# Graph network on Trainium2: in the gate layer, gather two of eight edge tiles on TensorE instead of by indirect DMA

## What is computed

```python
edge_input = jnp.concatenate([x[src], edge_attr], axis=-1)          # 100000 x (96 + 32)
messages = _gelu(edge_input @ mW1 + mb1) @ mW2 + mb2
gates = jax.nn.sigmoid(_gelu(edge_input @ gW1 + gb1) @ gW2 + gb2)
aggregated = jax.ops.segment_sum(messages * gates, dst, num_segments=x.shape[0])
update = _gelu(jnp.concatenate([x, aggregated], -1) @ uW1 + ub1) @ uW2 + ub2
# then x + update, layer norm, scale and shift
```

## Time and profile before

| what | us |
|---|---|
| median of 3 runs (3452.3 to 3453.14) | 3453.06 |
| the profiled execution | 3451.42 |
| its span, first to last instruction | 3449.7 |
| busy in the span: PE / DVE / POOL / ACT | 2703.8 / 2096.9 / 1316.5 / 692.8 |
| gate layer, from its first POOL instruction to the end of the span | 2371.2 to 3449.7 |
| 784 gathers on POOL (L1282): busy, and idle before them | 757.6, 243.8 |

### The profile page before, as it was taken

The page is one execution under the profiler, slowest core; times in us unless marked ns, Lnnn a source line. Parts: engine busy times, 40 slices in busy tenths (PEclk is TensorE's granted clock), DMA queues, the critical chain, the costliest instruction groups (busy, mean ns, idle before and its releaser), DMA issues.

```text
span 3449.7 us, 65375 instructions
## 1 busy us (share of the span) xinstructions
PE 2703.8 (78%) x22345; PEld 2109.0 (61%) x22346; DVE 2096.9 (61%) x4939; ACT 692.8 (20%) x1119; POOL 1316.5 (38%) x1350
## 2 busy tenths in 40 slices
PE   3677777999999989887999999985667765666764
PEld 0121111899999987776999999973445443444442
DVE  6888777823323472347988888874454545454545
ACT  0134455500000040111111111111111111111111
POOL 0000000000000000004777777753777777777772
PEclk9999999799999989998999999986776678776676
DMA  0000000000000000003544454522333333333331
GB/s 28 0 0 0 0 0 0 3 2 2 2 2 2 2 5 1 1 6 84 131 118 117 116 118 116 118 56 72 90 92 90 91 90 92 90 92 90 90 89 24
DMA packets 106162, 182.80 MB, mean 53 GB/s; under 512 B 37382, under 2 KB 65595, under 8 KB 105914
## 3 DMA queue, kind: packets, MB, share of 16 engines
q0 software_dynamic: 54880, 103.65, 12.1%
q1 hardware_dynamic: 51033, 75.67, 8.1%
HBM read 174.42 MB, written 4.80 MB: 52 GB/s over the span
## 4 chain that ended last, share of the span: by engine, by line
POOL 34%; issue 11%; DVE 5%; PE 2%; DMA 1%; ACT 0%; DVEq 0%; POOLq 0%; ACTq 0%
POOL gate_rows L1282 22%; POOL msg_rows L946 12%; DVE pre_space L1021 2%; PE msg_sums L1143 1%; DVE msg_rows L1045 0%; DMA first_rows<-pre_space 0%; PE gate_sums L1453 0%; ACT msg_src_near L958 0%; DVE pre_space L1350 0%; DVE msg_rows L1041 0%; DMA msg_rows<-h_rows,all_src_i 0%; DMA msg_src_row<-src_rows 0%; PE msg_sums L1158 0%; DVE pre_space L1113 0%; DMA gate_rows<-first_rows,all_src_i 0%
## 5 line engine op out<-in xcount | busy, mean ns | idle before, releaser
L1282 POOL DMA_INDIRECT gate_rows<-first_rows,all_src_i x784 | 757.6, 966 | 243.8 <-issue 238.7
L933 POOL MEMSET msg_shift<- 125x1 f32 x1 | 0.1, 100 | 1587.4 <-POOLq L646 1587.4
L946 POOL DMA_INDIRECT msg_rows<-h_rows,all_src_i x539 | 537.3, 997 | 164.1 <-issue 163.5
L1143 PE MATMUL msg_sums<-msg_parts,pre_space 125*128 125x192 f16 x6125 | 531.9, 249 | 36.3 <-DVE pre_space L1021 36.3
L1143 PEld LDWEIGHTS msg_sums<-msg_parts,pre_space 125*128 125x128 f16 x6125 | 513.0, 99 | 43.4 <-DVE pre_space L1021 37.8
L1453 PE MATMUL gate_sums<-gate_onehot,gate_passed 128*97 128x64 f32 x1584 | 257.2, 347 | 357.2 <-DVE gate_onehot L1380 357.2
L576 PE MATMUL hop_sums<-dense_work,dense_counts 125*128 125x192 f16 x6250 | 521.9, 247 | 14.3 <-DVE dense_t L530 6.7
L576 PEld LDWEIGHTS hop_sums<-dense_work,dense_counts 125*128 125x128 f16 x6250 | 519.2, 98 | 16.8 <-DVE dense_t L530 7.3
L1453 PEld LDWEIGHTS gate_sums<-gate_onehot,gate_passed 128*97 128x97 f32 x1584 | 239.4, 256 | 440.6 <-DVE gate_onehot L1380 440.5
L1344 DVE TENSOR_TENSOR gate_rows<-gate_rows,gate_sums 128x1536 f32<-128x1536 f32 x98 | 171.9, 1755 | 450.6 <-DMA gate_rows<-first_rows,all_src_i 450.6
L419 PE MATMUL cnt_sums<-cnt_hot,cnt_near 128*128 x1000 | 347.6, 411 | 119.3 <-DVE cnt_hot L358 114.3
(11 more groups left out here) (240 smaller groups left out, 2788.5 us busy)
## 6 DMA issues: line engine op xcount, KB each, us to landing
msg_edge<-edges SPq DMA_DIRECT2D x98, 384.0 KB
msg_src_row<-src_rows SPq DMA_DIRECT2D x49, 312.5 KB
gate_edge<-edges SPq DMA_DIRECT2D x98, 128.0 KB, 2.1
gate_rows<-first_rows,all_src_i POOLq DMA_INDIRECT x784
msg_rows<-h_rows,all_src_i POOLq DMA_INDIRECT x539
first_rows<-pre_space SPq DMA_DIRECT2D x6, 375.0 KB
all_x<-x SPq DMA_DIRECT2D x1, 1171.9 KB
h_rows<-all_h SPq DMA_DIRECT2D x6, 187.5 KB
```

The source lines that it names most:

```text
L946: nc.gpsimd.indirect_dma_start(out=rows[:, r, k, :], out_offset=None, in_=table, in_offset=bass.IndirectOffsetOnAxis(ap=src_i[:, at:at + 1 ...
L1143: last = nc.tensor.matmul(got[group % 2][:, n, 0:2 * D], pick[:, c % 2, j, i * EP:(i + 1) * EP], parts[:, j, :], start=(j == 0), stop=(j = ...
L1282: nc.gpsimd.indirect_dma_start(out=rows[:, r, k, :], out_offset=None, in_=table, in_offset=bass.IndirectOffsetOnAxis(ap=src_i[:, at:at + 1 ...
```

## The change

Of the 8 tiles of a group only 6 (BY) are still gathered by POOL from the table. The other 2 (ON) are gathered on PE, two groups (4 tiles, 512 edges) at a time: the picks are now the moving operand, so that the result is h of the sources, transposed, 96 x 512. ACT copies it under the 32 edge features, which SP loads to rows 96 to 127 of the same buffer `inputs`. PE then multiplies this 128-row input by the whole first weights `w1` on top of a bias product. ACT reads these two tiles for Gelu straight from PSUM, in instructions of their own. The edge product of the other six tiles becomes 2 x 3 matmuls with 96 rows and 192 columns, into one set of 3 banks instead of two. The picks have one buffer, in two parts of 13 and 12 node tiles (CUT). `parts`, `middle`, `node_no` and `w1` move to or appear in memory that both layers share. In the convolutions the six semaphores of the weight and bias loads become one, so that the first use waits for all six loads.

```diff
 # convolutions
-            for i in range(3):
-                sp.dma_start(w_sb[:, i, :], weights[i]).then_inc(w_loaded[i], 16)
...
+                sp.dma_start(w_sb[:, i, :], weights[i]).then_inc(loaded, 16)
+                sp.dma_start(b_sb[:, i, :], biases[i].unsqueeze(0).to_broadcast([NP, D])).then_inc(loaded, 16)
...
-                pe.wait_ge(w_loaded[c], 16)
+                pe.wait_ge(loaded, 96)
 # gated_layer, SP
+            for c in range(2):
+                load_row(c)
+                load_on_edges(c)
             for group in range(SLOTS):
                 load_edges(group)
+            load_row(2)
             for group in range(SLOTS, NG):
                 sp.wait_ge(edge_mixed, group - SLOTS + 1)
                 load_edges(group)
+                c = group // 2 + 1
+                if group % 2 and c < NG // 2:
+                    load_on_edges(c)
+                if group % 2 and c + 1 < NG // 2:
+                    load_row(c + 1)
 # POOL
-                for k in range(GT):
+                for k in range(BY):
 # ACT
+            def collect(c):
+                act.wait_ge(gathered, 2 * (c + 1))
+                if c >= 2:
+                    act.wait_ge(on_mixed, 2 * (c - 1))
+                nc.scalar.activation(inputs[0:D, c % 2, :], collected[c % 2], ACT.Copy).then_inc(collected_out, 1)
             def activate(group):
...
+                act.wait_ge(on_mixed, group + 1)
...
+                nc.scalar.activation(gated[:, group % 2, BY:GT, :], product[:, :, D:2 * D], ACT.Gelu
+                                     ).then_inc(gate_in, 1)
...
+                nc.scalar.activation(passed[:, group % KEPT, BY:GT, 0:D], product[:, :, 0:D], ACT.Gelu
+                                     ).then_inc(on_used, 1)
+                act.wait_ge(added, group + 1)
+                nc.scalar.activation(gated[:, group % 2, 0:BY, :], r[:, :, D:2 * D], ACT.Gelu).then_inc(gate_in, 1)
...
+            widen(0)
+            widen(1)
+            nc.scalar.activation(parts[:, :, 0:D], h[:, :, :], ACT.Copy, scale=ROW_LIFT).then_inc(rounded, 1)
+            widen(2)
+            collect(0)
 # DVE
+            def make_picks(c, part):
+                j0, j1 = ((0, CUT), (CUT, NT))[part]
+                if part == 0:
+                    dve.wait_ge(widened, c + 1)
+                if c:
+                    dve.wait_ge(gathered, 2 * (c - 1) + part + 1)
+                for j in range(j0, j1):
+                    nc.vector.tensor_scalar(pick[:, j, :], src_near[:, c % 2, :], node_no[:, j:j + 1],
+                                            1.0 / ROW_LIFT, ALU.is_equal, ALU.mult).then_inc(picked, 1)
+            make_picks(0, 0)
+            make_picks(0, 1)
...
+            make_picks(1, 0)
+            make_picks(1, 1)
             for turn in range(NG + 2):
...
                 if turn > 1:
                     steps = make_onehots(turn - 2)
+                if (turn + 4) // 2 < NG // 2:
+                    make_picks((turn + 4) // 2, turn % 2)
 # PE
+                if group:
+                    pe.wait_ge(added, group)
+                for half in range(2):
+                    for k in range(3):
+                        last = nc.tensor.matmul(sums[:, k, 2 * D * half:2 * D * (half + 1)],
+                                                edge[:, group % SLOTS, half, :], we[:, 2 * D * k:2 * D * (k + 1)],
+                                                start=True, stop=True)
...
+            def collect(c, part):
+                pe.wait_ge(picked, NT * c + (CUT, NT)[part])
+                if c >= 2:
+                    pe.wait_ge(collected_out, c - 1)
+                for j in range(*((0, CUT), (CUT, NT))[part]):
+                    for i in range(2):
+                        last = nc.tensor.matmul(collected[c % 2], parts[:, j, i * D:(i + 1) * D], pick[:, j, :],
+                                                start=(j == 0 and i == 0), stop=(j == NT - 1 and i == 1))
+                last.then_inc(gathered, 1)
+            def mix_inputs(group):
+                c = group // 2
+                pe.wait_ge(collected_out, c + 1)
+                pe.wait_ge(on_edge_ready[c % 2], 16 * (c // 2 + 1))
+                if group:
+                    pe.wait_ge(on_used, group)
+                nc.tensor.matmul(product, ones[:, :], bias[:, :, :], start=True, stop=False)
+                for i in range(ON):
+                    at = (group % 2 * ON + i) * EP
+                    last = nc.tensor.matmul(product[:, i, :], inputs[:, c % 2, at:at + EP], w1[:, :],
+                                            start=False, stop=(i == ON - 1))
+                last.then_inc(on_mixed, 1)
...
             for turn in range(NG + 2):
                 if turn + 1 < NG:
                     mix_edges(turn + 1)
+                if (turn + 3) // 2 < NG // 2:
+                    collect((turn + 3) // 2, (turn + 1) % 2)
+                if turn + 1 < NG:
+                    mix_inputs(turn + 1)
                 if turn > 1:
                     sum_messages(turn - 2)
```

More of the change, by code:

```diff
@@ L654, in convolutions @@
         sums = m.ps("sums", [128, 8, BANK], F32)
-        w_loaded = [m.sem(f"w_loaded{i}") for i in range(3)]
-        b_loaded = [m.sem(f"b_loaded{i}") for i in range(3)]
+        loaded = m.sem("loaded")
         chain = m.sem("chain"); normal = m.sem("normal")
@@ L919, in _ @@
                     sp.wait_ge(pre.we_cleared, 1)
-                    for k in range(4):
+                    for k in range(3):
                         at = 2 * D * k
@@ L1244, in gated_layer @@
         edge_ready = [m.sem(f"edge_ready{r}") for r in range(SLOTS)]
+        on_edge_ready = [m.sem(f"on_edge_ready{i}") for i in range(2)]
+        row_loaded = [m.sem(f"row_loaded{i}") for i in range(2)]
+        widened = m.sem("widened"); picked = m.sem("picked"); gathered = m.sem("gathered")
+        rounded = m.sem("rounded"); split = m.sem("split"); bias_set = m.sem("bias_set")
+        collected_out = m.sem("collected_out"); on_mixed = m.sem("on_mixed"); on_used = m.sem("on_used")
         edge_mixed = m.sem("edge_mixed"); added = m.sem("added"); rows_used = m.sem("rows_used")
@@ L1273, in _ @@
             nc.gpsimd.memset(passed[:, :, :, D:D + 1], 1.0).then_inc(made, 1)
+            nc.gpsimd.memset(ones[:, :], 1.0).then_inc(made, 1)
+            nc.gpsimd.memset(bias[:, :, :], 0.0).then_inc(made, 1)
             for i in range(2):
@@ L1319, in _ @@
                     open_gates(turn - 1)
+                if turn % 2 and (turn + 5) // 2 < NG // 2:
+                    widen((turn + 5) // 2)
+                if turn % 2 == 0 and (turn + 2) // 2 < NG // 2:
+                    collect((turn + 2) // 2)
             for q, (m0, n) in enumerate(GROUPS):
@@ new lines, in _ @@
+            link(nc.vector.tensor_copy(bias_part[:, 1, :], bias_rest[:, 0, :]))
+            link(nc.vector.tensor_tensor(bias_rest[:, 1, :], bias_rest[:, 0, :], bias_part[:, 1, :], ALU.subtract))
+            for k in range(ON):
+                link(nc.vector.tensor_copy(bias[0:1, k, :], b1[0:1, :]))
+                link(nc.vector.tensor_copy(bias[32:33, k, :], bias_rest[32:33, 0, :]))
+                link(nc.vector.tensor_copy(bias[64:65, k, :], bias_rest[64:65, 1, :]))
+            dve.sem_inc(bias_set, 1)
@@ L1337, in add_edges @@
             def add_edges(group):
                 turn, r = divmod(group, RING)
-                dve.wait_ge(rows_ready[r], 16 * GT * (turn + 1))
+                dve.wait_ge(rows_ready[r], 16 * BY * (turn + 1))
                 dve.wait_ge(edge_mixed, group + 1)
-                to = rows[:, r, :, :].rearrange("p k d -> p (k d)")
-                b = 3 * (group % 2)
-                products = sums[:, b:b + 3, :].rearrange("p b w -> p (b w)")
+                to = rows[:, r, :, :].rearrange("p (h k) d -> p h k d", h=2)
@@ L1344, in add_edges @@
+                products = sums[:, 0:3, 0:4 * D].rearrange("p k (h d) -> p h k d", h=2)
                 nc.vector.tensor_tensor(to, to, products, ALU.add).then_inc(added, 1)
@@ L1436, in mix_edges @@
                 pe.wait_ge(edge_ready[group % SLOTS], 16 * (group // SLOTS + 1))
-                if group >= 2:
-                    pe.wait_ge(added, group - 1)
-                b, wide, split = 3 * (group % 2), 4 * 2 * D, BANK // 2
-                for half, bank, to, frm, end in ((0, b, 0, 0, BANK), (0, b + 1, 0, BANK, wide),
-                                                 (1, b + 1, split, 0, split), (1, b + 2, 0, split, wide)):
-                    last = nc.tensor.matmul(sums[:, bank, to:to + end - frm], edge[:, group % SLOTS, half, :],
-                                            we[:, frm:end], start=True, stop=True)
@@ L1458, in _ @@
             mix_edges(0)
+            pe.wait_ge(joined_out, 2)
+            pe.wait_ge(split, 1)
+            collect(0, 0)
+            collect(0, 1)
+            pe.wait_ge(bias_set, 1)
+            mix_inputs(0)
+            collect(1, 0)
```

102 lines of the change are left out of this document (72 added, 30 removed).

## The result

The changed kernel takes 3400.39 us (median of 4 runs, 3395.86 to 3404.56) against 3452.68 us for the kernel before in runs beside it: ratio 0.9847, 95% interval 0.9835 to 0.986, about 53 us faster. The forecast was 3392 us. The profiled execution took 3397.08 us (3390.4 forecast), with a span of 3394.9 us and a granted clock of 0.95 over the whole.

A forecast was written before the change was run, and what follows sets the result against it. The gate layer was taken as bound by POOL's issue, 8 x 1.27 us a turn, then by PE. 63.5 us gained less 2.5 in the convolutions gave 61 off 3451.42: 3390.4, median 3392 us, range 3356 to 3432.

The forecast's parts named there:

- What sets the turn: Gate layer loop: PE sets the turn at 9.46 us, 9.54 with the clock allowance; PE never waits, DVE waits 0.3 us.
- The allowance of 0.08 us for half-clock spells: Gate layer loop: 0.08 us added to each PE turn for short spells at half clock.
- The price of a gather matmul: Gate layer, PE: a 512-column matmul costs 0.216 us, so half of 50 take 5.40 us a turn.
- the rival of a cheap PE: 512-column matmuls stream faster, so DVE's 9.15 us sets the turn: 36 us less, 3356 us; chance 0.05.
- DVE's turn: Gate layer loop: DVE needs 9.15 us a turn, with 12.5 picks of 0.285 us, 3.56 us in all.
- off the path as forecast: Gate layer, POOL: six gathers at 0.995 us busy beside picks, with their pauses, stay under 7.8 us a turn.
- The clock: Gate layer loop: PE has no gap, so its granted clock is near 1, at least 0.97.
- the slower rival: PE waits for DVE in its stretch without gathering, the clock falls to 0.83, turn 11.4 us: 3565 us; chance 0.11.
- The end: Last `add_edges` at 3318.4; after it 5.5 us gained as POOL's long additions run some seven turns earlier, 0.4 by shorter add.
- The start: Start of the gate layer: split done at 2387.0, 50 gather matmuls until 2400.3, PE's turn 0 at 2407.5.
- The 2.5 us for the half clock: Start of the gate layer: 50 gather matmuls take 10.8 us and 2.5 more, since PE was idle and begins at half clock.
- The convolutions: Start of the convolutions: waiting for all six loads costs 2.5 us on PE's path.

The follow-up runs named there:

- e4: Changed kernel with every second DVE pick of the gate layer left out (13 of 25 made): 3396.89 us, 0.9849 of the kernel before.
- e7: Changed kernel with POOL gathering five tiles of six from the eighth group on: 3400.82 us, 0.985 of the kernel before.
- e3: Changed kernel with PE's gathering halved, only the high fp16 part of h multiplied: 3337.82 us, 0.9676 of the kernel before.
- e5: Changed kernel with one tile of eight gathered on PE and seven by POOL: 3351.39 us, 0.9708 of the kernel before.
- e9: Changed kernel with three tiles of every sixteen gathered on PE and five buffers of `passed`, not six: 3307.31 us, 0.9584 of the kernel before.
- e1: Changed kernel with POOL's two long additions moved ahead of its gathers: 3400.27 us, 0.9863 of the kernel before.
- e8: Changed kernel with POOL's two long additions cut into 25 small pairs during the loop: 3397.53 us, 0.9835 of the kernel before.
- e2: Changed kernel with PE at first waiting for the first weight load alone in the convolutions: 3398.02 us, 0.9843 of the kernel before.

## Why the prediction came out as it did

**What sets the turn: right.** PE does, at 9.562 us (9.54 forecast). Its pauses are gone, and `add_edges` waits for PE. Leaving out picks (e4) and gathers (e7) leaves the turn as it is, leaving out half of PE's gathering doesn't (e3). Single terms: edges 2.01 us (1.93), gathering 25 x 0.216 = 5.40 (5.40), inputs 0.64, bias 0.17 (0.16), sums 1.35 (1.33). That sums to 9.57. The allowance of 0.08 us for half-clock spells wasn't needed, the clock being 1.00; the edge products took its place by 0.08. Over the 93 turns the difference is 93 x 0.022 = 2.0 us.

**The price of a gather matmul: right.** 24 in 5.18 us is 0.216 us. The Trainium skill, "TensorE: Matmul & The Clock Gate", section "Back-to-back issue gap", has both numbers: about 131 ns sustained, and about 216 ns as the formula for the isolated gap at N=512, which it says over-counts. Here the stream with a weight load for each matmul runs at the second, so the rival of a cheap PE had no ground.

**DVE's turn: near, and covered.** In the 650 us of 68 turns DVE waits 35.1 + 10.0 us for PE, 0.66 us a turn, so its own turn is about 8.90 us (9.15 forecast), with 0.289 us a pick (0.285). When PE's gathering is halved, DVE sets a turn of 8.96 us.

**POOL: off the path as forecast, but dearer.** Its gathers take 437.3 / 409 = 1.069 us and not 0.995; six with pauses of 0.30 are 8.2 us where "under 7.8" stood. e7 shows it off the path. In e5 and e9, where it sets the turn, the same term is the turn: 1.305 and 1.331 us a gather with its pause, against the 1.27 without picks beside it.

**The clock: right.** No gap in the loop, and 1.00. What gaps do is in e3 (0.90) and e5 (0.93): neither turn runs away, as the slower rival wanted. That rival was reckoned with 0.83 for the loop before; over the loop it was 0.72.

**The end: this step failed in its size.** I took 5.5 us for the hold that POOL's additions put on DVE, as they held L1350 before, and thought that DVE could be 6 us late before PE must wait. Before, the two additions came one behind the other as well, and this is the first:

```profile
3372.85 5.27 POOL L1287 TENSOR_TENSOR pre_space<-all_h,pre_ub 125x2400 f32<-125x2400 f32 x1
```

DVE stood waiting for gathered rows in most of it. Then `add_edges`, which has one operand in PSUM, ran from 3375.98 us on beside its end in its usual 1.75 us, and only L1350, with both operands in SBUF, was held, by the second. Now DVE has twelve picks in a row, and both additions hold them: 14.06 - 3.70 = 10.4 us. The forecast took the hold that one instruction met before for the hold of what stands there now. PE waited 3.70 us and then lost 3.27 - 2.17 + 5.99 - 5.34 = 1.75 us at a lower clock, in sum 5.45; moving the additions away gave the loop 5.7 us (e1) and 5.5 us (e8). The Trainium skill, "SBUF — State Buffer", section "Who interferes with whom", calls the port pair of DVE and GpSimd an exclusive lock; the 10.4 us for two additions of 5.27 and 5.26 agree with that, and the prediction had used only one of them. The 6 us that DVE may be late was sized well: a hold of 10.4 us made PE wait 3.70 us, the rest of 6.7 us was covered. The gain in the tail that the step names did come: the tail is 66.7 us against 73.7 before, 7.0 less, where 5.9 was forecast.

**The start: 2.4 us late.** From the layer's first instruction to PE's turn 0 it took 38.7 us, and 36.3 was forecast. The widening began at 2378.48, nearly 2 us later than I had it, waiting for a row that was the first load to be issued, and 25 picks took 7.74 and not 7.0 us. The 2.5 us for the half clock behind PE's pause had no row: the 50 matmuls took 12.95 us, 2.15 more than at full clock, and 12.5 to 13.95 us in the traces of e1 and e2, so this term scatters by more than 1 us.

**The convolutions: right in place and size** (5.99 - 3.24 = 2.75 us against 2.5), and the stage ends 2.6 us later than before, 302.59 against 299.97 us. That the gate layer began at 2371.15 us all the same, where 2373.7 was forecast, is scatter of that execution: the mean over seven traces is 2374.23.

So the account closes inside the gate layer. Forecast from its first instruction to the end of the span were 3388.7 - 2373.7 = 1015.0 us, measured 1023.75: the start 2.4, the additions 5.6, the turns 2.0, the tail -1.1, sum 8.9 us of 8.75. That is what separates the medians, 3392 and 3400.4; the profiled execution lay 3.3 us under its median, and its gate layer began 3.1 us before the mean. By the 2 us of scatter in the layer, the terms of 2 us are near, not exact. The causes of the start's parts are read from the trace alone.

## What to carry to other kernels

Write the turn of every engine beside the others as a sum of instructions, and choose the split where the largest sum is smallest: here 6, 7 and 6.5 gathers of eight gave 9.56 (PE), 9.13 (POOL) and 8.66 us (POOL, with PE 97% busy). That PE was busy 100% of the time in the first of them only said which sum was the largest, not that it was as small as it can be. Price an instruction beside the neighbours that it will have, for when two engines hold each other, either sum can pay. And work that hides costs nothing only as long as its engine isn't the bound: the same 50 small additions took 5.5 us off the loop in one split and put 20 us on it in the next.

## What the runs showed of the hardware that was not expected

Two long additions on POOL (5.27 and 5.26 us) held fp16 picks on DVE for both of their times, and no pick got through between the two: one lasted 11.10 us. Beside the first addition before, `add_edges`, with one operand in PSUM, took its usual 1.75 us; that the operand's place is the reason was not tried. Cut into 50 pieces of about 0.4 us the additions held nothing that can be seen in PE's turn. A gather's mean time on POOL grew from 0.967 us with no picks in the loop to 1.000 beside 256-wide, 1.026 beside 384-wide and 1.069 us beside 512-wide ones. The median is 0.946 to 0.949 us in all of these loops, so a few long gathers make the mean. Nor is the width all of it. Beside the same 512-wide picks the gathers took 403.1 / 406 = 0.993 us in e3, and there the picks took more, 255.6 / 838 = 0.305 us against 0.289; in e7 the gathers took 1.158 us and the picks less, 231.6 / 851 = 0.272 us. How the two engines fall together seems to decide who pays; that was not tried further. Over 600 us of the loop the granted clock was 0.91 where PE waited 50 times for 1.5 us in 67 turns (e3), 0.93 where it waited 58 times for 1.7 us in 66 turns (e5), and it was 0.72 in the loop before, where PE was busy for 560 of 850 us. So the time spent idle doesn't give the clock by itself.
